# Relative attention on one core: scores built twice, once natural for the row maximum and once turned in PSUM for the exponential, from fp16 pairs on two row tiles of TensorE

## The reference, cut to what matters

```python
Q = (x @ Wq.T + bq)...; K = (x @ Wk.T + bk)...; V = (x @ Wv.T + bv)...      # 16 heads of 16
rel_pos = arange(L)[None, :] - arange(L)[:, None] + 255                        # L = 2048
rel_k = relative_k[rel_pos]; rel_v = relative_v[rel_pos]                       # clipped / wrapped index
scores = einsum('bhld,bhrd->bhlr', Q, K) * scale + einsum('bhld,lrd->bhlr', Q, rel_k)
attn = softmax(scores)
out = einsum('bhlr,bhrd->bhld', attn, V) + einsum('bhlr,lrd->bhld', attn, rel_v)
```

## Time and profile before

| what | us |
|---|---|
| median of 3 runs (lowest, highest) | 4175.11 (4165.85, 4184.01) |
| the profiled execution, its own time | 4160.9 |
| its span, first to last instruction | 4159.6 |
| PE busy | 3599.3 (87%) |
| DVE busy | 3312.0 (80%) |
| ACT busy | 2952.8 (71%) |
| POOL busy | 2954.0 (71%) |
| `project`, until the first load of `attend` | 0 to 159.0 |
| the 512 Exps of `attend` start | 179.8 to 3559.4 |

### The profile page before, as it was taken

One profiled execution on the slowest core, in us unless ns is written; L12 is line 12 of the kernel. 1 busy time (PEld: TensorE's weight loads), 2 busy tenths in 40 slices (PEclk: granted clock), 3 DMA queues, 4 the chain that ended last, 5 costly groups with the idle time before them and its releaser, 6 DMA issues. The chain is left out here.

```text
span 4159.6 us, 173466 instructions
## 1 busy us (share of the span) xinstructions
PE 3599.3 (87%) x60310; PEld 3086.1 (74%) x60310; DVE 3312.0 (80%) x9926; ACT 2952.8 (71%) x4828; POOL 2954.0 (71%) x3233
## 2 busy tenths in 40 slices
PE   7689889898989898988888889898988999699991
PEld 4377777777777777777777777777777788558990
DVE  7598989888988888888898888888888989644443
ACT  3488878787878787878787878787778888325440
POOL 3488878787878787878787878787878887560005
PEclk9799999999999999999999999999999999759995
DMA  7755555555555555555555555555555555461224
GB/s 257 238 180 173 178 165 180 162 170 163 175 164 175 167 174 165 175 169 174 176 175 170 175 168 175 165 173 166 173 165 175 178 173 179 158 205 57 62 65 129
DMA packets 385646, 693.17 MB, mean 167 GB/s; under 512 B 62986, under 2 KB 190739, under 8 KB 383619
## 3 DMA queue, kind: packets, MB, share of 16 engines
q1 hardware_dynamic: 378498, 663.88, 49.9%
q0 software_dynamic: 6144, 16.79, 1.2%
HBM read 336.76 MB, written 343.49 MB: 164 GB/s over the span
## 5 line engine op out<-in xcount | busy, mean ns | idle before, releaser
L819 POOL TENSOR_TENSOR pt_near<-pt_full,pt_near 128x512 f16<-128x512 f32 (+3 forms) x2176 | 2069.5, 969 | 614.2 <-DVE pt_near L1089 598.3
L1057 DVE CUSTOM_DVE_ANT_0 scores<-pb,skewed 128x512 f32<-128x512 f32 (+3 forms) x2592 | 1396.3, 574 | 455.3 <-PE pb L857 222.1
L1013 ACT COPY pt_full<-pb 128x512 f32<-128x512 f32 x2048 | 1156.4, 585 | 543.1 <-PE pb L870 503.3
L870 PE MATMUL pb<-ident,scores 128*128 128x128 f32 x8192 | 1282.7, 280 | 50.0 <-issue 49.4
L1089 DVE CAST pt_near<-pt_full 128x512 f16<-128x512 f32 (+3 forms) x2176 | 1195.9, 592 | 0.3 <-ACT pt_full L1013 0.3
L870 PEld LDWEIGHTS pb<-ident,scores 128*128 128x128 f32 x8192 | 1031.2, 146 | 183.5 <-issue 63.1
L917 PEld LDWEIGHTS pb<-pt_near,table_high 128*128 128x128 f16 x18432 | 924.4, 97 | 254.9 <-issue 119.4
L917 PE MATMUL pb<-pt_near,table_high 128*128 128x64 f16 (+6 forms) x18432 | 993.9, 188 | 134.3 <-POOL pt_far L819 68.9
L1004 ACT ACTIVATE scores<-scores,exp_bias 128x2048 f32<-128x2048 f32 x512 | 1026.9, 2006 | 54.2 <-DVE exp_bias L1071 52.7
L917 PE MATMUL pb<-pt_near,table_low 128*128 128x64 f16 (+6 forms) x9216 | 945.1, 188 | 0.0
L857 PE MATMUL pb<-k_stack,q_stack 96*128 96x512 bf16 x2048 | 800.3, 391 | 45.7 <-DVE part_max L1057 43.3
(11 more groups left out here) (170 smaller groups left out, 3373.9 us busy)
## 6 DMA issues: line engine op xcount, KB each, us to landing
rel_scratch<-rel SPq DMA_DIRECT2D x896, 256.0 KB, 2.3
skewed<-rel_scratch SPq DMA_DIRECT2D x256, 576.0 KB, 4.0
rel_scratch<-rel SPq DMA_DIRECT2D x288, 128.0 KB, 2.1
skewed<-rel_scratch SPq DMA_DIRECT2D x64, 512.0 KB, 4.2
skewed<-rel_scratch SPq DMA_DIRECT2D x64, 448.0 KB, 4.1
planes_scratch<-planes SPq DMA_DIRECT2D x32, 384.0 KB, 2.7
q_stack<-planes_scratch SPq DMA_DIRECT2D x192, 64.0 KB, 3.9
k_stack<-planes_scratch SPq DMA_DIRECT2D x192, 64.0 KB, 4.3
```

The lines of the kernel that those rows point to most:

```text
L819: ins = nc.gpsimd.tensor_tensor(pt_piece(c, 1, a, z, near), pt_full[e][:, (a - 4 * g) * P:(z - 4 * g) * P], pt_piece(c, 0, a, z, near), AL ...
L870: ins = nc.tensor.transpose(t_ps[g % 2][:, i * P:(i + 1) * P], scores[u % 2][:, blk * P:(blk + 1) * P], keep["ident"][:, :])
L1013: nc.scalar.copy(pt_full[e][:, :], t_ps[ACT_GROUPS[e] % 2][:, :]).then_inc(s_ea, 1)
L1057: ins = nc.vector.tensor_tensor_reduce(out=scores[k % 2][:, a:z], in0=ps[:, a - bank * CH:z - bank * CH], in1=other, scale=1.0, scalar=-3. ...
```

## The change

`project` now forms fp16 pairs (high, low) straight out of PSUM: ACT writes the high part (one activation with bias), DVE the low part. There are four sources instead of two: Q, and three kinds of K (MID, LEFT, RIGHT); LEFT and RIGHT have the end row of the relative table in their bias, so that a far block's scores come out complete. `planes` are 4 x 2 of fp16 instead of 2 x 3 of bf16. POOL has nothing to do there.

In `attend`, a stack has three pairs of fp16 parts (48 rows) twice, at partitions 0 and 64: the row tiles. Keys 0 to 1023 use the lower tile, the others the upper. Before the first load, four memsets of 32 x 3072 on POOL and two of 128 x 2048 on DVE set the stacks' other rows, and SP waits for them. A unit then goes this way:

- PE, `rel_products`: two products of 384 columns, one on each row tile. ACT copies them out. SP stores them in one or two pieces, waits until they are stored and reads them back in the same step (before: one step later). `skewed` has four buffers.
- PE, `score_banks`: natural scores, far parts against LEFT or RIGHT keys, on the two row tiles in turn. DVE, `search_bank`: in the band the sum with `skewed` and its maximum (written as bf16 to a tile nobody reads), in the far parts a `tensor_reduce` out of PSUM. DVE writes the maximum as two fp16 columns (`maximum_high`, `maximum_low`).
- PE, `max_rows`: two matmuls of 128 columns put the query block and the two rows of the maximum into PSUM; ACT, `query_rows`, copies them to `q_max`.
- PE, `turned_scores`, two pairs of groups: the near blocks of `skewed` are transposed in fp32 straight into the bank (7.5 a unit), then 16 matmuls of 50 rows and 128 columns, keys stationary, `q_max` moving, add the scores less the maximum, the two row tiles in turn.
- ACT, `exponentials`: four Exps of 512 columns out of PSUM to `pt_full`. No row sum: the values get a column of ones (33 columns in place of 48), and DVE takes the reciprocal of it.
- The high parts of two groups are DVE's, of the other two ACT's (5.06 pieces in all, 2.5 and 2.56). The low parts stay on POOL, the 32 value matmuls, the 54 relative ones and the picks on PE. The splitting of V on POOL takes 8 instructions a head in place of 14.

Gone are the 16 transposes of the probabilities, their four copies and the long Exp. The groups are taken in the order 0, 2, 1, 3. The cut diff:

```diff
-LAG_SKEW, LAG_S, LAG_E, LAG_T, LAG_PV = 2, 3, 4, 5, 6
+LAG_S, LAG_A, LAG_X, LAG_PV = 2, 3, 4, 5
-LAG_O = LAG_SEL + 4
+LAG_O = LAG_SEL + 1
-ACT_GROUPS = (0, 1, 2, 3)
+GROUP_ORDER = (0, 2, 1, 3)
 def bank_items(k):
+    return [("scores", k - LAG_S, 0), ("scores", k - LAG_S, 2), ("rel", k, 0), ("rel", k, 1),
+            ("scores", k - LAG_S, 1), ("scores", k - LAG_S, 3), ("max", k - LAG_A, 0)]
-BANKS = 3
+BANKS = 4
...
+                    nc.scalar.activation(planes[:, v, 0, :], source(kind, half)[:, :], ACT.Identity,
+                                         bias=bias_of(kind, half)).then_inc(s_hi, 1)
...
+                    nc.vector.scalar_tensor_tensor(planes[:, v, 1, :], source(kind, half)[:, :], bias_of(kind, half),
+                                                   planes[:, v, 0, :], ALU.add, ALU.subtract).then_inc(s_pl, 1)
...
+            sp.wait_ge(s_kset, 4)
             load_stacks(sp, 0, 0)
...
+                    sp.wait_ge(s_ge, it * (2 * STEP) + 2 * u + 2)
+                    for to, a, w in rel_pieces(u % NB):
+                        sp.dma_start(hbm["rel_scratch"][u % 2, :, to:to + w], rel[u % 2][:, a:a + w]).then_inc(s_gw[u % 2], 16)
                     sp.wait_ge(s_gw[u % 2], stored(it, u))
...
-                    sp.dma_start(skewed[u % 2][:, 0:w], skew_src(u % 2, w)).then_inc(s_gr[u % 2], 16)
+                    sp.dma_start(skewed[u % 4][:, 0:w], skew_src(u % 2, w)).then_inc(s_gr[u % 4], 16)
...
+            def max_rows(it, u):
+                pe.wait_ge(s_nm, it * STEP + u + 1)
+                wait_bank(it, "max", u, 0)
+                nc.tensor.matmul(ps, max_parts[u % 2][:, :], ident_half[:, :], start=True, stop=False)
+                nc.tensor.matmul(ps, ident_half[:, :], q_stack[b][:, c * P:(c + 1) * P],
+                                 start=False, stop=True).then_inc(s_mt, 1)
+            def turned_scores(it, u, pair):
+                if pair == 0:
+                    pe.wait_ge(s_q, it * STEP + u + 1)
+                for e in steps:
+                    if 4 * u + e >= 2 and (near[e] or e % 2):
+                        pe.wait_ge(s_exp, it * (4 * STEP) + 4 * u + e - 1)
+                    for blk in near[e]:
+                        nc.tensor.matmul(x_ps[e % 2][:, (blk - 4 * g) * P:(blk - 4 * g + 1) * P],
+                                         skewed[u % 4][:, col:col + P], keep["ident"][:, :], is_transpose=True,
+                                         start=(blk == near[e][0]), stop=False)
                 for i in range(4):
+                    for e in steps:
+                        ins = nc.tensor.matmul(x_ps[e % 2][:, i * P:(i + 1) * P],
+                                               k_stack[b][tile_rows(tile, STACK + 2), kind_of(c, blk), col:col + P],
+                                               q_max[u % 2][tile_rows(tile, STACK + 2), :],
+                                               start=(i == 0 and not near[e]), stop=(i == 3))
...
             def step(it, k):     # tensor
+                for pair in range(2):
+                    turned_scores(it, k - LAG_X, pair)
+                    score_banks(it, k - LAG_S, pair)
+                    if pair == 0: rel_products(it, k)
+                    values(it, k - LAG_PV, 2 * pair)
+                    values(it, k - LAG_PV, 2 * pair + 1)
+                max_rows(it, k - LAG_A)
+                for quarter in range(4):
+                    rel_values(it, h, j, quarter)
...
             def step(it, k):     # scalar
+                    exponentials(it, k - LAG_X, 0)
+                    exponentials(it, k - LAG_X, 1)
+                    for n in range(2):
+                        rel_evac(it, k, n)
+                    exponentials(it, k - LAG_X, 2)
+                    exponentials(it, k - LAG_X, 3)
+                    high_part(it, k - LAG_X, 2)
+                    high_part(it, k - LAG_X, 3)
+                    query_rows(it, k - LAG_A)
...
             def step(it, k):     # vector, after the half head's output, read-out and masks
+                    search_bank(it, a, 0)
+                    search_bank(it, a, 2)
                     high_part(it, t, 0)
                     high_part(it, t, 1)
+                    search_bank(it, a, 1)
+                    search_bank(it, a, 3)
                     raw_maximum(it, a)
+                    maximum_high(it, a)
+                    maximum_low(it, a)
```

More of the change, by code:

```diff
@@ L64, in blocks, with rel_pieces @@
     return hi - lo + 1
[L67 to L73, removed]
+PERIOD = 2 * MAXLEN - 1
+RELN = 6 * P
+WRAP = 5 * P
+SAME0 = P + 1
+def rel_pieces(c):
+    lo, hi = window(c)
+    first, last = (lo - M_LO) * P, min((hi + 1 - M_LO) * P + P, RELW - 1)
+    out = []
+    for a, z, back in ((first, min(last, WRAP), 0), (max(first, WRAP), last, PERIOD)):
+        if a < z:
+            out.append((a - first, a - back, z - a))
+    return out
 STEP = 2 * NB
@@ L192, in sem @@
             return ctx.enter_context(nc.semaphore(name))
-        FULL = ((0, 0), (0, 1), (1, 0), (1, 1))
+        FULL = [(0, half) for half in range(2)] + [(1 + kind, half) for kind in range(KINDS) for half in range(2)]
         NFULL = len(FULL)
@@ L380, in _ @@
                                     base=DK * SHIFTS - 1, pattern=[[-DK, SHIFTS]], channel_multiplier=-1).then_inc(s_id, 1)
-            def step(gg, par, first, last):
-                g = gg * 2 + par
-                for v in range(NFULL):
-                    pool.wait_ge(s_mid, g * NFULL + v + 1)
-                    pool.nop(nofuse=True)
-                    nc.gpsimd.tensor_tensor(planes[:, v, 2, :], rest[:, v, :], planes[:, v, 1, :],
-                                            ALU.subtract).then_inc(s_pl, 1)
-            chunks(pool, step)
         @block.scalar
@@ L794, in v_part @@
                     pool.nop(nofuse=True)
-                parts = v_head[b][:, version, :, :, :]
+                high, low = (v_head[b][:, version, :, i * DK:(i + 1) * DK] for i in range(2))
                 full = v_full if version else v_in[b]
@@ new lines, in high_part, with query_rows @@
+            def high_part(it, u, e):
+                c, g = u % NB, GROUP_ORDER[e]
+                act.wait_ge(s_exp, it * (4 * STEP) + 4 * u + e + 1)
+                wait_pt_free(act, it, u, e)
+                for a, z, near in pieces(c, g):
+                    ins = nc.scalar.copy(pt_piece(c, 0, a, z, near), pt_full[e][:, (a - 4 * g) * P:(z - 4 * g) * P])
+                ins.then_inc(s_ha, 1)
+            def query_rows(it, u):
+                act.wait_ge(s_mt, it * STEP + u + 1)
+                if u >= 2:
+                    for s in s_x:
+                        act.wait_ge(s, it * (2 * STEP) + 2 * (u - 1))
+                nc.scalar.copy(q_max[u % 2][:, :], bank_of("max", u, 0)[:, 0:P]).then_inc(s_q, 1)
```

510 lines of the change are left out of this document (249 added, 261 removed).

## The result

The changed kernel takes 4265.64 us (median of 4 runs, 4251.61 to 4282.15), the kernel before 4176.48 (4 runs, 4165.85 to 4184.01). The ratio is 1.0217, with a 95% interval of 1.0172 to 1.0261: slower by 2.2%, where 3890 us was forecast. The profiled execution took 4251.61 us, of them 4250.4 in its span.

A forecast was written before the change was run, and what follows sets the result against it. The prediction took a PE-DVE loop as the bound, replaced by ACT's 4.6 us chain plus 1.23 waiting for PE plus 0.15: 6.0 us a unit against 6.61. With +27 outside and 14 for the median: 3890 us, range 3740 to 4110.

The forecast's parts named there:

- the SP and DMA bullet: Band stores and read in `attend`: 8.6 of 10.3 us needed; SP's queue, with its waits and stack loads, under 6.0 us.
- The chain from scores to search: Relative scores ready 3.2 us into a step, search at 13.5: two stores and a read need 8.6 of 10.3 us.
- The band comes late: Rival: store plus read over 10.3 us, or SP's queue over 6.0, makes DVE's search wait; 4150 to 4250 us, chance 3%.
- The old loop: PE's relative products and DVE's third bank in `attend`: 4.2 us of DVE plus 2.6 of PE, 6.84 us, broken by the change.
- ACT's chain: ACT's work per unit in `attend`: Exps, relative copies, high parts and query rows, 5.37 us summed, 4.6 us with overlap.
- DVE's sum: DVE per unit in `attend`: 5.7 us before; half the casts removed, a third small operation adding 0.2; 5.0 to 5.3.
- Tiles at once: Eight turned matmuls on two row tiles in `attend`: 0.22 us if at once (chosen), 0.44 if one after the other.
- From the full array to tiles: PE's change of arrangement before the turned matmuls: between nothing and 0.17 us, with 0.17 chosen.
- My lower bound of 5: `project`, taken as bound by stores: larger planes cost 16 us more at 270 GB/s, bounds 5 to 20.
- 0.15 for what happens once in eight units: Per-unit addition in `attend` for eight picks in one burst (0.88 us on PE), output and read-out.
- the loop's terms: ACT's idle time awaiting PE's turned scores: semaphore 0.05, transposes 0.78, matmuls 0.22, change 0.17; stated sum 1.23, bounds 1.05 to 1.45.
- The clock: Rival: PE's granted clock, 0.97 before, falls; at 1.2 GHz PE's work doubles to 9 us, 5400 us, chance 3%.

The follow-up runs named there:

- kernel 4: Changed kernel with the wait and band read of a unit issued one step later, after the next unit's stores, all later lags one longer: 3953.25 us, ratio 0.949.
- kernel 7: Read-one-step-later variant of the changed kernel, with every product reading its rows from the lower row tile: 4229.72 us, ratio 1.0151.
- kernel 2: Changed kernel with stack and V loads issued between the stores and the wait for them: 4126.98 us, ratio 0.9906.
- kernel 1: Changed kernel with the band read from another HBM region, same size, without waiting for the stores: 3972.76 us, ratio 0.9521.
- kernel 9: Changed kernel with stores whole and waited for, the read cut to 16 columns from another region: 3924.49 us, ratio 0.9425.
- kernel 10: Changed kernel with whole band reads from another region, each store cut to 16 columns and still waited for: 3965.09 us, ratio 0.9523.

## Why the prediction was wrong

The step that failed is the SP and DMA bullet: "Two stores ... 2 x 2.3, and a read of 3.9 need 8.6 of the 10.3 there are. SP ... is held 4.6 + 0.4 for the read, and in 6 units of 16 another 0.8 for stack loads: under 6.0 too."

- *What it was held.* The 2.3 us came from stores of 256 KB in a queue that waited for them only a step later, and that issued them only after the read before had landed. With up to 640 KB the hold measured 2.9 to 4.7 us in blocks 1 to 6, about what I gave it, and 5.1 to 6.4 where SP was late; the read, the issues and the stack loads behind it took 1.5 rather than 1.2. So where it mattered SP's cycle was 6.8 us, not 5.8. 6.8 is also past the 6.6 of before, and this is why the sign turned.
- *Why a margin of 0.2 was none.* I compared 5.8 with 6.0 as two constants. The hold depends on the gap, and the gap on the hold; once SP is late it stays late (c = 7 to 15 above). The chain from scores to search has the same flaw: by an estimate from these rows, a hold of 5.5 and a read of 4.6 are 10.1 of the 10.3, before SP's own lateness is added.
- *The rival* "The band comes late" was the true case, with 3% given to it. Its time, 4150 to 4250, was 16 us too low. It named SP's queue "over 6.0" as a condition, but priced only the chain: "all of the gain only from 11.6 us on". SP's own cycle gives the gain back from 6.6 us on.
- *What it cost.* With the read a step later (kernel 4) a unit takes 6.18 instead of 6.78: 0.60 x 512 = 307 us, and the medians differ by 312.

Right, point by point:

- The old loop is gone and ACT's chain plus PE's turned scores is the new one: 5.66 to 5.71 us against 5.83 in an undisturbed step, 5.85 as the mean of 13 query blocks in kernel 4.
- ACT is busy 661.8 x 6.78 / 1000 = 4.5 us a unit (chain forecast 4.6), POOL 5.0 (5.0), DVE 5.25 (5.0 to 5.3). In DVE's sum two terms were off and nearly cancelled. The two operations on 2 columns take 0.575 + 0.856 us in place of one of 0.15, 1.28 more, where I gave 0.2. The casts fell from 2.75 us a unit (1407.5 us over 512) to 0.87 (444.6), 1.88 less, where I took 0.9 off.
- Tiles at once: 0.23 and 0.22 us against the 0.22 and 0.22 chosen (kernel 7: 0.46 with one tile). From the full array to tiles: four transposes take 2008.57 - 2007.98 = 0.59 to the start of what follows, against 4 x 0.11, so 0.15 of change where 0.17 was chosen. Here the Trainium skill (TensorEngine Tiling (Array Packing), Key Properties), which says that different tiles load and multiply in parallel, agrees with the trace.
- The memsets on POOL take 10.8 us (11). `project` lost some 3 us, not 16: it moves 295 GB/s at a share of 0.89 where I kept 270 GB/s. My lower bound of 5 was nearer.

Off in size: "0.15 for what happens once in eight units". The eight picks are 16 records and take 1.94 us at the full clock, not 0.88: the 0.11 us that I took from the earlier trace rows was for one record of two. In kernel 4 the two blocks with picks and output add (1.29 + 1.69) / 16 = 0.19 us a unit. Left out, without a reason: what PE stands at the program's loop, in the kernel before as well. In kernel 4 block 2 adds 2.25 / 16 = 0.14 us a unit by it. So a unit takes 5.85 + 0.33 = 6.18 and not 6.0, 92 us in all, of which the cheaper `project` gives 13 back. This, not the band, is why the mended kernel reaches 3953 us (3940 with one column for the maximum) and not 3890. Both beat the kernel before, by 5.1% and 5.6%.

Two slips in the sums change nothing: the loop's terms add up to 1.22, not 1.23, and its bounds of 1.05 to 1.45 give 5.80 to 6.20 us a unit, where the range was taken from 5.75 to 6.35.

The clock: in the changed kernel it is 0.91 from 1000 to 2000 us, in kernel 4 0.97. In the disturbed place shown above it fell behind PE's waits. From 1014 to 1016 us PE was busy 1.17 us of 2 at a granted clock of 1.00, and from 1017 to 1026 the clock was 0.50; the mean over ten us:

```profile
1014.00:1024.00 10.00, 9.04 (x111) 7.87 (x111) 6.43 (x19) 3.54 (x8) 5.32 (x7) 0.64 0.58 184
```

A granted clock of 0.64 is a mean of the two levels, 2.4 and 1.2 GHz, and the 16 picks took 3.57 us instead of 1.94. This was so for 10 of the 64 bursts of picks in the changed kernel and for none in kernel 4. So part of the 312 us is the slower clock that came with the waits. From 1000 to 2000 us it was 0.94 in kernel 2, 0.95 in kernel 1, 0.96 in kernels 9 and 10; how much of the time it is was not separated.

## What to carry to other kernels

Cost a DMA queue that is issued in order like an engine with a loop of its own: issue, landing where the queue waits for it, and everything issued behind that wait. A landing time is only good with the same traffic ahead of it, and in a loop whose length grows when it is late, the 3% between 5.8 and 6.0 us were no margin. Give a read of what was just stored a step of lag, so that the queue waits for the stores of the unit before. And list what the kernel does once per turn of its loop: it is in the measured period, but not in the step that one reads off a timeline.

## What the runs showed of the hardware

- A store of 320 KB landed in 2.5 to 3.1 us where the queue did not issue it right behind a large read (kernels 1, 4 and 9), and in 4.1 to 4.6 us right behind reads of 576 KB in the changed kernel. Stores cut to 8 KB held the queue for 2.1 or for 4.5 us (kernel 10).
- Matmuls on two row tiles need not be issued in turn: four on one tile and then four on the other pass in the same 0.23 us as alternating ones.
- PE stood 3.2 to 6.7 us at each of the 13 jumps back of the loop over 32 units, in the kernel before, the changed one and kernel 4 alike, with no wait that the profile shows.
- DVE's two operations on 2 columns took 0.575 and 0.856 us in the mean of the changed kernel. In its first two units, with POOL idle from 187.2 to 197.6 us, each took 0.17; in the next, beside POOL's subtractions, 0.59 and 1.07:

```profile
190.56 0.17 DVE L1123 TENSOR_SCALAR max_parts<-neg_max 128x2 f16<-128x2 f32 x1
190.76 0.17 DVE L1128 SCALAR_TENSOR_TENSOR max_parts<-neg_max,max_parts 128x2 f16<-128x2 f32 x1
...
197.63 3.57 POOL L832 TENSOR_TENSOR pt_near<-pt_full,pt_near 128x384 f16<-128x384 f32 x4 [10.43 <-DVE pt_near L1137]
200.14 1.07 DVE L1128 SCALAR_TENSOR_TENSOR max_parts<-neg_max,max_parts 128x2 f16<-128x2 f32 x1
```

The trace has no other such operation with POOL idle, and no run takes POOL's work away; so that POOL makes them wait is likely, not shown. The reduce just before them, which forms the maximum, took 0.16 us in all three.
